# Moving the maxima's transpose behind the first value projection, and padding the factors' rounded halves to 128 rows

## The reference

```python
q = split_heads(x_q @ Wq + bq) * dp_scale
k = split_heads(x_kv @ Wk + bk)
v = split_heads(x_kv @ Wv + bv)
attn = softmax(where(causal_mask, neg, einsum('bhic,bhjc->bhij', q, k)))
o = einsum('bhij,bhjc->bhic', attn, v) ; x = x + o @ Wo + bo
```

## Time and profile before

| | us |
|---|---|
| median of 3 runs | 1711.04 (1706.59 to 1711.32) |
| profiled execution | 1706.42 |
| its span | 1704.6 |
| PE busy | 1598.4 (94%) |
| PE weight loads busy | 1368.8 (80%) |
| DVE, ACT, POOL busy | 1021.9 (60%), 954.9 (56%), 697.8 (41%) |

### The profile page before, as it was taken

The page is one execution under the profiler, slowest core; times in us unless marked ns, Lnnn a source line. Parts: engine busy times, 40 slices in busy tenths (PEclk is TensorE's granted clock), DMA queues, the critical chain, the costliest instruction groups (busy, mean ns, idle before and its releaser), DMA issues. The chain is left out here.

```text
span 1704.6 us, 48946 instructions
## 1 busy us (share of the span) xinstructions
PE 1598.4 (94%) x20162; PEld 1368.8 (80%) x20179; DVE 1021.9 (60%) x1427; ACT 954.9 (56%) x1834; POOL 697.8 (41%) x625
## 2 busy tenths in 40 slices
PE   7999999999887999999999887998699999999987
PEld 5888888888655888888888776976488888888863
DVE  7667777775356777667777343013676666666632
ACT  4677777777413465666565612311267777777752
POOL 5655555551004555554554000000375555555302
PEclk9999999999998899999999989989999999999998
DMA  7675555554135676555555353970465555555440
GB/s 178 172 191 130 123 131 131 131 127 101 59 115 130 177 200 152 141 138 138 141 141 121 79 204 116 323 267 36 102 171 149 135 132 131 132 128 130 103 116 4
DMA packets 149247, 235.45 MB, mean 138 GB/s; under 512 B 24200, under 2 KB 64516, under 8 KB 148100
## 3 DMA queue, kind: packets, MB, share of 16 engines
q1 hardware_dynamic: 141090, 225.09, 50.5%
q10 hardware_dynamic: 7938, 7.23, 1.5%
HBM read 107.06 MB, written 0.23 MB: 63 GB/s over the span
## 5 line engine op out<-in xcount | busy, mean ns | idle before, releaser
L1304 DVE TENSOR_REDUCE L_xattn_maxima<-L_xattn_ps 128x4 f32<-128x1024 f32 x588 | 691.3, 1219 | 340.2 <-PE L_xattn_ps L877 336.4
L1066 ACT ACTIVATE L_xattn_p_ring<-L_xattn_ps 128x512 f32<-128x512 f32 x1176 | 677.5, 598 | 304.0 <-PE L_xattn_ps L926 288.6
L926 PE MATMUL L_xattn_ps<-L_xattn_q_packed,L_xattn_k_packed 128*128 128x256 f32 x2352 | 458.5, 299 | 8.6 <-ACT L_xattn_p_ring L1066 4.7
L926 PEld LDWEIGHTS L_xattn_ps<-L_xattn_q_packed,L_xattn_k_packed 128*128 128x128 f32 x2352 | 338.8, 190 | 65.0 <-issue 29.6
L962 PE MATMUL L_xattn_ps<-L_xattn_p_ring,L_xattn_v_ring 128*17 128x128 f32 x9408 | 289.3, 273 | 1.0 <-ACT L_xattn_p_ring L1066 1.0
L1238 POOL TENSOR_TENSOR L_xattn_k_ring<-L_xattn_k_full,consts 128x512 fp32r<-128x512 f32 x147 | 155.1, 1055 | 279.6 <-ACT L_xattn_k_full L1079 159.3
L845 PE MATMUL L_xattn_ps<-L_xattn_ctx_halves,L_xattn_w_halves 128*128 128x256 f32 x1764 | 262.0, 287 | 0.5 <-POOL L_xattn_ctx_halves L1223 0.5
L962 PEld LDWEIGHTS L_xattn_ps<-L_xattn_p_ring,L_xattn_v_ring 128*17 128x17 f32 x9408 | 242.4, 97 | 23.6 <-ACT L_xattn_p_ring L1066 1.6
L849 PE MATMUL L_xattn_ps<-L_xattn_w_halves,L_xattn_ctx_halves 128*128 128x256 f32 x1764 | 260.8, 286 | 0.0
L845 PEld LDWEIGHTS L_xattn_ps<-L_xattn_ctx_halves,L_xattn_w_halves 128*128 128x128 f32 x1764 | 234.3, 194 | 3.7 <-issue 1.9
L849 PEld LDWEIGHTS L_xattn_ps<-L_xattn_w_halves,L_xattn_ctx_halves 128*128 128x128 f32 x1764 | 233.6, 193 | 2.2 <-issue 0.4
(11 more groups left out here) (377 smaller groups left out, 1143.3 us busy)
## 6 DMA issues: line engine op xcount, KB each, us to landing
L_xattn_k_packed<-L_xattn_k_ring SPq DMA_DIRECT2D x588, 128.0 KB, 2.4
L_xattn_ctx_chunk<-in_ctx_chunks SPq DMA_DIRECT2D x147, 256.0 KB, 3.2
L_xattn_k_packed<-L_xattn_k_ring SPq DMA_DIRECT2D x588, 64.0 KB, 2.1
L_ffn_W<-in_experts_W SPq DMA_DIRECT2D x16, 1024.0 KB, 13.6
L_xattn_mask_chunk<-L_xattn_mask ACTq DMA_DIRECT2D x49, 128.0 KB, 3.1
weights<-in_pack_L_attn SPq DMA_DIRECT2D x10, 512.0 KB, 4.8
L_xattn_ctxT<-in_ctxT SPq DMA_DIRECT2D x5, 896.0 KB, 8.1
L_xattn_ctx<-in_ctx SPq DMA_DIRECT2D x5, 896.0 KB, 8.2
```

The lines of the kernel that those rows point to most:

```text
L926: last = pe.matmul(L.ps[:, bank, d * 2 * S:(d + 1) * 2 * S], self.k_packed[s][:, quarter, d, half * P:(half + 1) * P], q[:, 2 * pair:2 * p ...
L1066: act.activation(self.p[t % P_RING][:, 4 * quarter:4 * quarter + 4, :], L.ps[:, E_BANK[unit], :].rearrange("p (h n) -> p h n", n=S), ACT.Exp)\
L1304: dve.tensor_reduce(out[:, 4 * v:4 * v + 4], L.ps[:, M_BANK + 2 * v:M_BANK + 2 * v + 2, :] .rearrange("p b (k n) -> p (b k) n", k=2), AX_X ...
```

## The change

Four edits in `CrossAttention`. T is called on PE after the first half of the value projection (`pe_project(..., 2)`) and before s5, where it stood behind the attend and before s3. `turned_before` gives 5 for all steps of the full loop, so ScalarE copies T between s4 and s5, and the banks alternate in that order. `stage_T` and `spread` get 128 rows in place of 64 and 32; rows 64 to 127 of `stage_T` are zeroed once by VectorE, `spread` is 0 on rows 32 to 127, and F multiplies all 128 rows. PE waits once for the zeroing.

```diff
@@ turned_before
-    return 3 if step < NCHUNK else 5
+    return 3 if step < LAG else 5
@@ sizes
-        self.spread = ... "spread", [2 * H, H, 32], F32R
+        self.spread = ... "spread", [P, H, 32], F32R
-        self.stage_T = sb("stage_T", [64, S], F32R)
+        self.stage_T = sb("stage_T", [P, S], F32R)
@@ pe_factor
-                             self.stage_T[0:2 * H, :], start=True, stop=True, skip_group_check=True)
+                             self.stage_T[:, :], start=True, stop=True, skip_group_check=True)
@@ tensor
+        pe.wait_ge(L["stage_T_padded"], 1)
...
                 self.pe_attend(pe, m - 1, 1)
-                if b is not None:
-                    self.pe_turned(pe, b)
                 self.pe_unit(pe, m, 3)
                 self.pe_unit(pe, m, 4)
                 self.pe_project(pe, step, 2)
+                if b is not None:
+                    self.pe_turned(pe, b)
                 self.pe_unit(pe, m, 5)
@@ act_turned
-        act.activation(self.stage_T[:, :], L.ps[0:64, E_BANK[unit], 0:S], ACT.Copy).then_inc(L["e_drained"], 1)
+        act.activation(self.stage_T[0:64, :], L.ps[0:64, E_BANK[unit], 0:S], ACT.Copy).then_inc(L["e_drained"], 1)
@@ vector
         dve.memset(self.stage[:, 0:32], 0.0)
+        dve.memset(self.stage_T[64:P, :].bitcast(F32), 0.0).then_inc(L["stage_T_padded"], 1)
```

More of the change, by code:

```diff
@@ L166, in __init__ @@
         self.zeros_bf = ctx.enter_context(nc.sbuf_tensor("zeros_bf", [P, BANK], BF16))
-        self.spread = ctx.enter_context(nc.sbuf_tensor("spread", [2 * H, H, 32], F32R))
+        self.spread = ctx.enter_context(nc.sbuf_tensor("spread", [P, H, 32], F32R))
         self.x = ctx.enter_context(nc.sbuf_tensor("x_rows", [S, D], F32))
@@ L1121, in make_constants @@
             dve.tensor_copy(net.ident_bf[:, :], identity).then_inc(L["constants_made"], 1)
-            dve.tensor_tensor(net.spread[:, :, :], wide(identity[0:2 * H, 0:H], 32), wide(identity[0:2 * H, H:2 * H], 32),
+            dve.tensor_tensor(net.spread[:, :, :], wide(identity[:, 0:H], 32), wide(identity[:, H:2 * H], 32),
                               ALU.add).then_inc(L["constants_made"], 1)
```

## The result

The changed kernel takes 1699.99 us (median of its five runs), against 1711.04 (1706.59 to 1711.32). Four of the five lie from 1693.46 to 1701.02; the fifth, of 3687.53, with nothing like it in any other kernel here, is left out of the comparison. The ratio is 0.9932, 95% interval 0.991 to 0.9953. The change makes the kernel faster by 0.5 to 0.9%. I had forecast 1707.2 (1701.8 to 1713.9) and, as most likely (0.51), no difference that can be measured. The profiled execution takes 1697.52 where before it took 1706.42: 8.9 us less, where my sum had 3.8.

The account below looks back on a forecast made before the run. TensorE's queue, busy 94% of the span, was taken as the bound; 19 steps at -0.01, 10 at -0.26 and a late one at -1.0 made -3.8 us, from 1711.04 to 1707.2 (range 1701.8 to 1713.9).

Parts of the forecast that it names:

- the read of s4: Turned steps of L0_xattn and L3_xattn: ScalarE has read s4 at 1.74 us, so s5 loads at 1.79.
- F's read at s7: L0_xattn and L3_xattn: ScalarE's copy of F holds s7 until 4.21 us against 4.22 before, -0.01 in 19 steps.
- L1: Turned steps of L1_xattn: s7 loads at 4.20 us instead of 4.46, not held by F, -0.26 ten times.
- rival (a): L0_xattn and L3_xattn: F's reading does not hold s7, -0.14 instead of -0.01 in 19 steps, 1704.7 us; chance 0.27.
- The late shift: Fifth turned step of L0_xattn's full loop: T's wait of 1.22 us for VectorE goes, -1.01.
- The padding: F at full height in turned steps: s5 to s6 takes 1.41 us instead of 1.75.
- rival (b): At F's edges: padding gives nothing, s6 stays 1.75 us behind s5, +3.6, 1714.6 us; chance 0.11.
- The move: Turned steps of L0_xattn and L3_xattn: T before s5 alone is 0.20 us worse, s5 at 1.79 instead of 1.59.
- SP and POOL: Behind the moved T: SP issues the shift load 1.31 us later, POOL waits 1.31 more for its context chunk; cost 0.
- rival (c): At the next step's s0: shift columns land late, 0.23 us past its turn, +2.9, 1713.9 us; chance 0.06.

Follow-up runs that it names:

- `memset_only`: The kernel before with `stage_T` of 128 rows, its zeroing and PE's wait for it, F still reading 32 rows: 1707.65 us, ratio 1.0.
- `pad_only`: The changed kernel with T back at its old place before s3, so F padded alone: 1698.38 us, ratio 0.9945 to the kernel before.
- `half_f_copy`: The changed kernel with ScalarE taking the exponential of only 256 of F's 512 columns: 1699.02 us, ratio 0.9951 to the kernel before.
- `move_only`: The kernel before with T moved to before s5, F still on 32 rows: 1706.0 us, ratio 1.0001.
- `pad64`: The kernel before with F on 64 rows instead of 32, and 64 rows in `spread`: 1708.26 us, ratio 1.001.
- `t_s5`: F at full height, T moved behind s5, ScalarE's copy of T before that of the projected values: 1701.46 us, ratio 0.9961 to the kernel before.

## Why the prediction was wrong

**The accounts of the loops.** Before to `memset_only` -1.2, on to `pad_only` -9.0, on to the changed kernel +1.8 by the move: -8.4. My -3.8 was too small by ScalarE's read of s4 above all (some 3 of the 4.6 that were missing), and by two smaller things.

- **The step that failed: the read of s4, and so F's read at s7.** I took three reads in 1.79 as two equal gaps of 0.595, so that s4 was read at 1.74. In the changed kernel it is read at 1.64. The same view cut to shorter windows takes such a row apart. The ordinary step at 134.10 of the kernel before, and last the one that I had read:

```profile
134.10 1.09 ACT L1066 ACTIVATE L_xattn_p_ring<-L_xattn_ps 128x512 f32<-128x512 f32 x2 [1.18 <-PE L_xattn_ps L926]
...
135.30 0.60 ACT L1066 ACTIVATE L_xattn_p_ring<-L_xattn_ps 128x512 f32<-128x512 f32 x1
...
118.25 1.18 ACT L1066 ACTIVATE L_xattn_p_ring<-L_xattn_ps 128x512 f32<-128x512 f32 x2 [1.18 <-PE L_xattn_ps L926]
```

s3's and s4's reads start 0.49 apart, and s5's comes 0.71 later, when its own matmuls are done: the length of the merged row is set by s5 and says little on s4. In the step that I had picked the gap was 0.58, so my 0.595 was nearly right for it, but it is one of only six among the 93 ordinary steps of the kernel before where the gap is above 0.50; the others have 0.49 to 0.50, and so have all 30 turned steps of the changed kernel. Two of my own rows said so: the gap of 0.50 that I used from V to s6, and s4's read at 1.04 in L1_xattn, where my chain for L0 put it at 1.145, though the work up to there is the same. L1, forecast from the right row, came out right. So s5 loads at 1.69, not 1.79; V and F's copy follow (0.10, and 0.03 more on the way), and s7 stands at 4.08, not 4.21. That is rival (a)'s size (-0.14) and its reason (ScalarE ahead of my count), though the hold that (a) wanted gone is there, as `half_f_copy` shows. The projection behind s7 follows at 4.30 where it was at 4.44, and the whole step measures -0.18; 19 such steps are 3.4 us instead of my 0.2. Since s7 waited 0.12 for the copy, every hundredth on ScalarE's chain up to it went straight into the step: there a sum must hold to 0.05, and I had priced a merged row.
- **Seven of L0's steps gained 0.25, not 0.18.** Before, they took 9.20 to 9.22, since where VectorE dequantizes the first batch comes some 0.06 later (3.08 to 3.09 behind the second, elsewhere 3.03). With F padded, s7 waits for its copy and the first batch stands 3.14 behind the second everywhere, with T at either place, so this is hidden: 7 x 0.07 = 0.5. `move_only`, with 9.20 and 9.27, shows that the move does not hide it.
- **The late shift: -1.26 and -0.35 where I had -1.0.** The wait did go, and `move_only` shows that the move alone hides a stage as late as that (10.22 to 9.27, with the stage ready 0.89 behind the attend). But in the changed kernel the stage was not late, so the move had nothing to hide: that this term came out near its size was luck. The late stage itself was a coincidence of a hundredth, and the zeroing, which I had priced at 0 to +0.8, goes with 0.35 less in the step ahead.
- **L1: right**, -0.27 for -0.26.
- **The padding: right in mechanism and size**, 1.39 for 1.41, and rival (b) false; `pad64` closes it.
- **The move: right that alone it is worse**, but 0.10 at s5 and 0.06 to 0.07 at the step's end, not 0.20. I had not asked for the obvious consequence, that the padding without the move is better than both.
- **SP and POOL: right**, and rival (c) false here, though `t_s5` shows its wait once the shift load is issued 0.6 later.
- **Weighing.** I set the sum on the median of before, 1711.04, which is some 4 above the medians of that kernel in all three later groups. That cost part of the distance; by the profiled executions it is 1702.6 against 1697.5, still 5.1 off. The range went only 0.8 below that 1702.6, too little for a sum whose largest term, 19 steps, hung on a hold of 0.13.

## What to carry to other kernels

A merged row of back-to-back reads gives their spacing only if none of them waited for its own input; cut the window so that it comes apart, and check it in more than one step. Where a hold is a tenth of a microsecond long, forecast both the held and the free case at comparable chance. Pad a short matmul to the whole array where it stands between whole-array ones, and test such a change one edit at a time: here the other edit gave back a fifth of its gain.

## What the runs showed that I had not expected

- In these steps leaving the full-height form costs PE 0.33 us for both edges together, at 64 rows just as at 32.
- Operations of 0.17 us on 128x16 elements on VectorE last until POOL's addition of 128x512 has ended (mostly 0.9 to 1.14) when they start 0.006 us or more behind its start, and are not slowed when they start 0.005 or less behind it; this caught 9 to 16 of the 36 executions of the last of them (L1325 before) in each profile. In one step of the kernel before it made T late by 1 us.
- With the zeroing at a layer's head (one small instruction more for VectorE, one wait more for PE) a reduction far behind it starts 0.34 us earlier, in the same step in every profile.
